# A fused recurrence and mixture-of-experts block on one core: decoder and output biases seeded by ScalarE, a router on differences of logits, experts in pairs, and a new order of stages

## The reference, cut to what matters

```python
xn = layernorm(x)
# s: the recurrence, one step per subsampled token
x_sub = rmsnorm(xn[:, ::2]) * g_norm
x_proj, gate = split(x_sub @ w_in.T + b_in)
h = tanh(h * A + x_proj[t][:, :, None] * Bm)        # h: (4, 512, 64), 2048 steps
y = h @ Cm.sum(0) + Dv * x_proj[t]
s = (y * silu(gate)) @ w_out.T + b_out
# g: the expert branch, on the same xn
cont = sigmoid(xn @ W_enc + b_enc) @ W_s2c + b_s2c  # 64 wide
top-2 of 8 experts by softmax(cont @ Wr + br), their weights renormalised
expert_out = sum_e gate_e * (relu(cont @ W1_e + b1_e) @ W2_e + b2_e)
g = silu(layernorm(sigmoid(expert_out @ W_c2s + b_c2s) @ W_dec + b_dec) * ln_g + ln_b)
out = x + s * g
```

## Time and profile before

| | us |
|---|---|
| median of 3 runs (6344.37 to 6348.86) | 6344.98 |
| the profiled execution | 6343.27 |
| its span, first to last instruction | 6341.6 |
| TensorE busy | 6147.9 (97%) |
| VectorE busy | 5732.7 (90%) |
| GpSimd busy | 5613.0 (89%) |
| ScalarE busy | 3988.1 (63%) |
| mean granted TensorE clock | 0.988 of full |

### The profile page before, as it was taken

One profiled execution on the slowest core, in us unless ns is written; L12 is line 12 of the kernel. 1 busy time (PEld: TensorE's weight loads), 2 busy tenths in 40 slices (PEclk: granted clock), 3 DMA queues, 4 the chain that ended last, 5 costly groups with the idle time before them and its releaser, 6 DMA issues.

```text
span 6341.6 us, 89178 instructions
## 1 busy us (share of the span) xinstructions
PE 6147.9 (97%) x29376; PEld 3202.8 (51%) x29376; DVE 5732.7 (90%) x10060; ACT 3988.1 (63%) x8390; POOL 5613.0 (89%) x3276
## 2 busy tenths in 40 slices
PE   5999999999999999999999999999999999999998
PEld 3555545555555455455554554555545545555554
DVE  4999999999999999999999999999999999999997
ACT  3666666666666666666666666666666666666665
POOL 4988989989889889899898898998988989989987
PEclk9999999999999999999999999999999999999999
DMA  5444444444434444444344444443444444444443
GB/s 144 104 110 99 110 105 104 110 102 107 110 99 110 105 103 110 102 107 112 97 110 106 103 113 102 105 113 95 109 108 102 114 101 106 112 96 110 109 102 80
DMA packets 157799, 672.95 MB, mean 106 GB/s; under 512 B 45589, under 2 KB 46613, under 8 KB 91799
## 3 DMA queue, kind: packets, MB, share of 16 engines
q1 hardware_dynamic: 157336, 667.24, 42.5%
HBM read 616.73 MB, written 50.33 MB: 105 GB/s over the span
## 4 chain that ended last, share of the span: by engine, by line
PE 91%; DVE 3%; POOL 3%; ACT 1%; issue 1%; SPq 1%; DMA 0%; POOLq 0%; DVEq 0%
PE bank L844 17%; PE bank L793 14%; PE ps_y L760 14%; PE ps_acc L856 9%; PE ps_acc L899 7%; PE bank L899 7%; PE bank L780 7%; PE bank L920 3%; PE bank L878 3%; PE bank L832 2%; POOL u L498 1%; PE bank L891 1%; PE ps_acc L891 1%; PE ps_acc L805 1%; PE ps_acc L878 1%
## 5 line engine op out<-in xcount | busy, mean ns | idle before, releaser
L498 POOL TENSOR_TENSOR u<-xb,bt 128x1024 f32<-128x1024 f32 x2048 | 4831.7, 2367 | 535.2 <-DVE ps_z L996 521.3
L600 ACT ACTIVATE h<-ps_z 128x512 f32<-128x512 f32 x4096 | 2377.1, 602 | 1280.0 <-DVE ps_z L996 1208.3
L990 DVE TENSOR_TENSOR ps_z<-h,ps_A 128x512 f32<-128x512 f32 x4096 | 2673.9, 691 | 416.0 <-ACT h L600 369.5
L996 DVE TENSOR_TENSOR ps_z<-ps_z,u 128x512 f32<-128x512 f32 x4096 | 2660.6, 691 | 8.7 <-POOL u L498 8.7
L844 PE MATMUL bank<-wide,w 65*128 65x256 f32 x4096 | 1138.8, 403 | 7.6
L760 PE MATMUL ps_y<-h,c_wide 128*32 128x512 f32 x8192 | 986.5, 599 | 0.0
L844 PEld LDWEIGHTS bank<-wide,w 65*128 65x128 f32 x4096 | 698.9, 189 | 454.6 <-issue 320.2
L793 PE MATMUL bank<-xnT,w_enc 128*128 128x256 f32 x4096 | 920.9, 383 | 6.5 <-ACT wide L623 6.5
L793 PEld LDWEIGHTS bank<-xnT,w_enc 128*128 128x128 f32 x4096 | 769.7, 190 | 213.0 <-issue 106.1
L681 ACT ACTIVATE hT<-bank 128x512 f32<-128x512 f32 x1024 | 604.1, 598 | 384.0 <-PE bank L844 366.6
L856 PE MATMUL ps_acc<-hT,w 128*64 128x256 f32 x4096 | 668.0, 404 | 6.7
(11 more groups left out here) (107 smaller groups left out, 4295.7 us busy)
## 6 DMA issues: line engine op xcount, KB each, us to landing
xb<-x_proj_scratch SPq DMA_DIRECT2D x2048, 256.0 KB, 4.5
xbuf<-in_L_attn_x SPq DMA_DIRECT2D x256, 128.0 KB
xres<-in_L_attn_x SPq DMA_DIRECT2D x512, 64.0 KB
out<-g SPq DMA_DIRECT2D x256, 128.0 KB
x_proj_scratch<-xp SPq DMA_DIRECT2D x256, 64.0 KB
w_in<-in_L_attn_w_in SPq DMA_DIRECT2D x1, 2048.0 KB
w_enc<-in_L_ffn_W_enc SPq DMA_DIRECT2D x1, 2048.0 KB
w_dec<-in_L_ffn_W_dec SPq DMA_DIRECT2D x1, 2048.0 KB
```

The costliest lines, as they stand in the source:

```text
L498: pool.tensor_tensor(u[:, tau % 2, :, :], xt, bt[:, :, :], ALU.mult).then_inc(u_ready, 1)
L600: act.activation(h[:, tau % RING, f, :], ps_z[:, f, :], ACT.Tanh).then_inc(h_ready, 1)
L990: dve.tensor_tensor(ps_z[:, f, :], h[:, (tau - 1) % RING, f, :], ps_A[:, f, :], ALU.mult).then_inc(m_done, 1)
L996: dve.tensor_tensor(ps_z[:, f, :], ps_z[:, f, :], u[:, tau % 2, f, :], ALU.add).then_inc(z_ready, 1)
```

## The change

Three pieces of work are done in another way, and most slots of the tables move.

1. `dec_seed` (ScalarE, slots 25 and 26) and `out_seed` (slot 37) copy the bias, now held on all 128 partitions, into the PSUM bank; the matmuls of `decode` and `fin_out` add to it, and their three bias matmuls are gone. TensorE waits for the seed.
2. `w_r` holds all 64 differences of the columns of `Wr` and the identity beside them. The router is one matmul of 128 columns per half of the tokens; its bias is one matmul of 256 columns over one row, issued in `controller` ahead of the sum. The copy of the logits is gone, and VectorE's routing has eight instructions instead of twelve, most of them of 64 columns.
3. `experts(p)` issues two ups, then the two downs of the pair before. The results of four `relu` are kept instead of two (the other two in the room of `conte`).
4. The tables: TensorE takes `gateT_transpose` ahead of the `conteT` ones, the others keep their order; VectorE, ScalarE, GpSimd and SyncE get other slots.

```diff
-SP_RESIDUAL = (36, 48)
+SP_RESIDUAL = (35, 47)
-POOL_GATE_MUL = -3
+POOL_GATE_MUL = -1
-POOL_FIN_SKIP = 31
-POOL_FIN_GATE = 36
-POOL_FIN_ADD = (53, 59)
+POOL_FIN_SKIP = 29
+POOL_FIN_GATE = 37
+POOL_FIN_ADD = (56, 62)
-ACT_LOGITS_COPY = 6.5
-ACT_ROUTE_SIG = 9.5
+ACT_ROUTE_SIG = 8.5
-ACT_DEC_SIG = (35.5, 39)
+ACT_DEC_SIG = (35.0, 38.5)
+ACT_OUT_SEED = 37
+ACT_DEC_SEED = (25, 26)
-PE_ROUTER = 8
-PE_CONTET = (17, 17, 18, 18)
-PE_GATET = 18
-PE_EXPERTS = (19, 19, 19, 19, 19, 19, 19, 19, 19, 19, 19, 20, 22, 22, 24, 28, 28)
-PE_TO_SPIKES = (31, 31, 31, 31)
+PE_ROUTER = 7
+PE_CONTET = (16, 17, 18, 18)
+PE_GATET = 15
+PE_EXPERTS = (19, 19, 19, 19, 19, 20, 22, 24, 28)
+PE_TO_SPIKES = (29, 29, 29, 29)
-DVE_PROJ_EVAC = (-21.25, -20.25)
-DVE_ROUTE = (7.25, 7.5, 7.75, 7.75, 8, 8.25, 9, 9.75)
-DVE_ROUTE_GATE = 10
-DVE_DEC_STATS = (28.75, 31.75)
-DVE_DEC_CENTRE = (30.75, 36.75)
+DVE_PROJ_EVAC = (-21.5, -20.5)
+DVE_ROUTE = (7.25, 7.5, 7.75, 8, 8, 8.25)
+DVE_ROUTE_GATE = 9.0
+DVE_DEC_STATS = (28.75, 31.0)
+DVE_DEC_CENTRE = (30.0, 36.75)
-DVE_FIN_Y = 34.75
-DVE_FIN_MUL = 40.5
+DVE_FIN_Y = 35.5
+DVE_FIN_MUL = 40.25
...
+            def dec_seed(blk, q):
+                if q == 0:
+                    wait_drained(act, (blk, C2S_FILL[1]))
+                else:
+                    act.wait_ge(acc_drained, 2 * blk + 1)
+                act.activation(dec_out[q][:, :], b_dec_all[:, :], ACT.Copy).then_inc(dec_seeded, 1)
+            def out_seed(blk):
+                wait_free(act, fin_fill(blk, FILL_FIN + 1))
+                act.activation(bank[1][:, :], b_out_all[:, :], ACT.Copy).then_inc(out_seeded, 1)
...
+                pe.matmul(ps_acc[:, T2:T2 + 2 * (E * E + M)], ones[96:97, :], br_row, start=True, stop=True)
...
                 for q in range(2):
                     tokens = contT[:, P * q:P * q + P]
-                    pe.matmul(logit_acc[:, q, :], ones[64:65, :], bias_rows[64:65, 0:E], start=True, stop=False)
-                    pe.matmul(logit_acc[:, q, :], tokens, w_r[:, :], start=False, stop=True)
-                    ins = pe.matmul(cont_acc[:, q, :], tokens, ident_2[:, :], start=True, stop=True)
+                    ins = pe.matmul(routed[:, q, :], tokens, w_r[:, :], start=False, stop=True,
+                                    skip_group_check=True)
...
-            def experts(blk, n):
-                if n < 16:
-                    expert_up(blk, n)
-                if n > 0:
-                    expert_down(blk, n - 1)
+            def experts(blk, p):
+                if p < 8:
+                    expert_up(blk, 2 * p)
+                    expert_up(blk, 2 * p + 1)
+                if p > 0:
+                    expert_down(blk, 2 * p - 2)
+                    expert_down(blk, 2 * p - 1)
...
             def decode(blk, q):
-                if q == 0:
-                    wait_free(pe, (blk, FILL_DEC))
-                else:
-                    pe.wait_ge(acc_drained, 2 * blk + 1)
+                pe.wait_ge(dec_seeded, 2 * blk + q + 1)
-                pe.matmul(dst[:, :], ones[0:1, :], bias_rows[0:1, :], start=True, stop=False)
...
             def fin_out(blk):
-                wait_free(pe, at)
-                pe.matmul(bank[1][:, :], ones[32:33, :], bias_rows[32:33, :], start=True, stop=False)
+                pe.wait_ge(out_seeded, blk + 1)
```

More of the change, by code:

```diff
@@ L154, in build @@
         ident = sb("ident", [P, P])
-        ident_2 = sb("ident_2", [P, M])
-        before = sb("before", [P, E, E])
+        least = sb("least", [P, E, E])
         c_wide = sb("c_wide", [P, F, 2 * SP - 4])
@@ L176, in build @@
         sg = sb("sg", [P, D])
-        logit = sb("logit", [P, 2, E])
         sel = sb("sel", [P, 2, E])
-        over = sb("over", [P, 2, E, E])
-        top_sum = sb("top_sum", [P, 2])
+        ahead = sb("ahead", [P, 2, E, E])
+        behind = sb("behind", [P, 2, E])
         gate = sb("gate", [P, 2, E])
@@ L207, in build @@
         gateT_acc = ps_acc[0:E, 0:T2]
[L208 to L216, removed]
+        routed = ps_acc[:, T2:T2 + 2 * (E * E + M)].rearrange("p (q n) -> p q n", q=2)
+        lead = [routed[:, q, 0:E * E].rearrange("p (e j) -> p e j", e=E) for q in range(2)]
+        cont_acc = routed[:, :, E * E:E * E + M]
+        rank = ps_acc[:, 0:16].rearrange("p (q e) -> p q e", q=2)
+        weight = ps_acc[:, 16:32].rearrange("p (q e) -> p q e", q=2)
         weights_loaded = sem("weights_loaded")
@@ L742, in between @@
                 for q in range(2):
+                    if slot == ACT_DEC_SEED[q]:
+                        dec_seed(blk, q)
+                for q in range(2):
                     if slot == ACT_DEC_SIG[q]:
                         dec_sig(blk, q)
+                if slot == ACT_OUT_SEED:
+                    out_seed(blk)
                 if slot == ACT_FIN_EVAC:
@@ L793, in encode @@
                         ins = pe.matmul(bank[n % 2][:, T2 * half:T2 * half + T2], w_enc[:, k, P * m:P * m + P],
-                                        xnT[:, par, k, :, :], start=(k == 0), stop=(k == KD - 1))
+                                        xnT[:, par, k, :, :], start=(k == 0 and half == 0), stop=(k == KD - 1),
+                                        skip_group_check=True)
                 filled(ins, at)
@@ L878, in to_spikes @@
                     ins = pe.matmul(dst[:, T2 * half:T2 * half + T2], w_c2s[:, P * m:P * m + P],
-                                    eoT, start=True, stop=True)
+                                    eoT, start=(half == 0), stop=True, skip_group_check=True)
                 if at:
@@ L961, in between @@
                     gateT_transpose(blk)
-                for n in range(17):
+                for n in range(9):
                     if slot == PE_EXPERTS[n]:
@@ L1018, in proj_evac @@
                                                  op0=ALU.mult, op1=ALU.add), at)
-            others = logit_acc.unsqueeze(2).to_broadcast([P, 2, E, E])
-            own = logit[:, :, :].unsqueeze(3).to_broadcast([P, 2, E, E])
-            earlier = before[:, :, :].unsqueeze(1).to_broadcast([P, 2, E, E])
             def route(blk, n):
                 if n == 0:
-                    dve.wait_ge(logits_copied, blk + 1)
+                    dve.wait_ge(logits_ready, blk + 1)
                     for q in range(2):
-                        dve.tensor_tensor(atleast[:, q], others[:, q], own[:, q], ALU.is_ge)
-                        ins = dve.tensor_tensor(over[:, q], others[:, q], own[:, q], ALU.is_gt)
+                        ins = dve.tensor_tensor(ahead[:, q], lead[q], least[:, :, :], ALU.is_ge)
@@ L1047, in route @@
-                if n == 7:
-                    ins = dve.scalar_tensor_tensor(out=margin, in0=logit_acc, scalar=2.0,
-                                                   in1=top_sum[:, :].unsqueeze(2).to_broadcast([P, 2, E]),
-                                                   op0=ALU.mult, op1=ALU.subtract)
+                    ins = dve.tensor_reduce(behind[:, :, :], ahead[:, :, :, :], AX.X, ALU.add)
                 ins.then_inc(route_steps, 1)
@@ L1129, in between @@
                         proj_evac(blk, par, half)
-                for n in range(8):
+                for n in range(6):
                     if slot == DVE_ROUTE[n]:
```

86 lines of the change are left out of this document (49 added, 37 removed).

## The result

The changed kernel takes **6539.67 us** (median of 4 runs, 6526.6 to 6556.09), the kernel before 6346.64 (4 runs, 6344.37 to 6348.86). The ratio is 1.0305, with a 95% interval of 1.028 to 1.0331. It is slower, where 6125 and a chance of 0.94 for faster had been forecast. The profiled execution took 6526.6 us.

A forecast was written before the change was run, and what follows sets the result against it. TensorE's matmuls were taken to set the pace, VectorE's recurrence close behind. Legs of 24.6, 20.6 and 48.7 us gave 93.9 per block against 97.35: 221 us saved over 64 blocks, 2 lost at the start, so 6125 us, range 5990 to 6225.

The forecast's parts named there:

- the one in the rivals: Clock rival, chance 0.04: TensorE's idle places bring 1.2 GHz stretches, 1.0 us each; six per block give 6508 us.
- leg A: Block part from the end of `dec_norm(1)` to the first `expert_up`: 26.0 us was to become 24.6.
- leg B: Block part from the first `expert_up` to `relu` 12: 22.5 us was to become 20.6.
- `fin_mul` now waits for VectorE's own order instead: In leg A, TensorE finishes `fin_out` about 2 us earlier and VectorE's routing, about 0.8 us shorter, sets `fin_mul`.
- `fin_mul` is one quarter slot earlier, which costs nothing: In leg A, moving VectorE's `fin_mul` a quarter slot ahead was counted as 0 us.
- Leg C: Block part from `relu` 12 to the next end of `dec_norm(1)`, paced by the recurrence: 48.8 us was to become 48.7.
- The wait at slot 28.75: In Leg C, VectorE's 0.41 us wait for the decoder's output was to go.
- two gaps stand behind the seeds: In Leg C, each decoder seed between two tanh was to delay its step by 0.4 us, 0.8 in all.
- GpSimd's side instructions: `fin_skip`, `fin_add` and `gate_mul`, moved to slots 29 to 31 ahead of the next block's u: 0.2 us lost.
- The 2 us for loading the bias rows: At the kernel's start, two bias rows become 128 rows, 0.5 MB more to load: 2 us estimated.
- The likeliest case: Chance 0.69: the recurrence takes over in Leg C and partly leg A; 92.4 to 94.9 us per block, 6030 to 6190.
- TensorE's own saving: TensorE's work falls by 6.3 us per block of 97.35, from bias matmuls, router and paired experts; 403 us if nothing else bound.

The follow-up runs named there:

- experiment 1: The changed kernel with the expert pairing alone undone, experts one by one again: 6443.96 us, 1.0158 of the kernel before.
- 4: The kernel before with the experts two by two alone, with four relu buffers: 6481.2 us, ratio 1.021.
- 3: The changed kernel with the ups over all 128 rows instead of 65, expert 0's result being another one: 6280.01 us, 0.9899 of the kernel before.
- 5: The kernel before with the experts two by two and the ups over all 128 rows, added rows zero: 6204.16 us, ratio 0.9779.
- 2: The changed kernel with two unread 128-row matmuls, one ahead of each of the first two pairs of ups: 6278.24 us, 0.9897 of the kernel before.
- 6: The kernel before with only the three bias matmuls replaced by ScalarE's seeds: 6366.59 us, ratio 1.0035.
- 7: The kernel before with only the router on differences of logits, the bias matmuls of decode and fin_out staying: 6387.82 us, ratio 1.0069.
- 8: The changed kernel with two unread 128-row matmuls ahead of the experts and GpSimd's second dec_silu ahead of u of step 8: 6168.27 us, 0.9725 of the kernel before.
- Experiment 9: The kernel of 8 with the three seeds moved behind the second tanh (slots 24.5, 26.5, 37.5): 6129.18 us, 0.966 of the kernel before.
- the three last runs: GpSimd's second dec_silu moved ahead of u of step 8 in the kernel of 6, the kernel before and the kernel of 5: 6512.48, 6444.09 and 6325.41 us.

## Why the prediction was wrong
**The step that failed first** is the one in the rivals: "A stretch at 1.2 GHz cost 1.0 us in the earlier trace rows", "so from four such stretches per block on it decides". The mechanism was named, its price was that of a stretch of 3.4 us in leg A, and its cause was looked for in idle places of TensorE. The prediction's count of such stretches was not what happened either: a short block of the changed kernel has one. The stretch that decided is one of 30.7 us. It costs 14.5 us in leg B (35.1 against 20.6), with the 6.8-us stretch that mostly goes ahead of it 16.8 in one block of three or four, 283 us over the kernel. It lies where TensorE has no idle time. Its conditions are the pairing (experiments 1 and 4) together with the 65 rows of the ups (3 and 5), and two matmuls over 128 rows at the head of the stage prevent it (2). The price of a 3.4-us stretch depends on its place: 1.0 us over `fin_out`, 1.7 over the input projection (6 and 7), nothing over the controller of the changed kernel. With GpSimd's wait gone (8) it costs 0.7 there too (leg A 25.47 against 24.76). Without the pairs, and so without the long stretch, the change is still slower than the kernel before (6444 us, experiment 1): the steps under leg A failed by themselves. The forecast of 6508 in this rival is near the measured time by luck: it stands for six short stretches per block, and TensorE's idle places were not the condition.

**Leg A: 24.6 forecast, 26.18 measured.** The step was "`fin_mul` now waits for VectorE's own order instead". It waits for GpSimd's, up to 1.66 us. The prediction read one block of before, one with a stretch at 1.2 GHz, in which TensorE was last by 1.1 us; in the 28 without one GpSimd's `dec_silu` was, so that TensorE's two microseconds could give 1.1 in half of the blocks and nothing in the others. Experiment 8, with GpSimd's order mended, gives 24.76. A second step failed beside it: "`fin_mul` is one quarter slot earlier, which costs nothing". It puts both sums of step 8 behind the wait for GpSimd, where one had stood ahead. In blocks without a stretch `fin_mul` starts 10.5 us after `dec_norm(1)` before, 10.4 in the changed kernel, but the last sum of step 8 ends at 12.43 and 13.05. With the seeds or the router alone, where `fin_mul` keeps slot 40.5, it ends at 12.38 and 12.41, and leg A is 25.50 and 25.53 against 26.18. So the quarter slot cost about 0.6 us per block; no run moves it back by itself. The terms beside it were near: the seed of 256 columns takes 0.60 us to the next group (3024.38 to 3024.98; forecast 0.57), and the seed ahead of the controller's sum starts within 0.2 us of the end of `dec_norm(1)`.

**Leg B: 20.6 forecast, 20.63 measured** where the clock is up. 0.3 us per pair was forecast, 0.31 measured (4).

**Leg C: 48.7 forecast, 48.83 measured.** The wait at slot 28.75 is gone; two gaps stand behind the seeds, 0.31 us each where 0.4 was forecast; `dec_norm(0)` does not wait for the stores. Experiment 9 shows what the seeds' places cost altogether, 0.7 us. Not every term is confirmed by the agreement: without the pairs the leg is 49.24 (1), with the seeds alone 48.67 (6), with the pairs alone 48.24 (4), so the pairs gave 0.4 to 0.6 here where 0.2 was counted, and other parts of the change took as much back; which, no run shows. The forecast also took 0.2 us for GpSimd's side instructions and left it out of its sum, which would be 48.9.

**Two smaller terms.** The 2 us for loading the bias rows had no row behind it; the blocks start 2.45 us later. The likeliest case's lower gain was not the sum of its legs' bounds: 1.0 and 1.4 less 0.8 is 1.6 us, 95.75 per block and not 94.9.

**TensorE's own saving**, 6.3 us per block forecast: 94.91 busy in the undisturbed block before, 88.77 after, 6.1 less. It is real and almost none of it is on the path: it becomes TensorE's idle time (6.9 us per block, 2.0 before), because the recurrence in C and GpSimd in A pace the block.

**What stays open.** Why one block in three or four falls into the long stretch, while the instructions and nearly the gaps in the expert stage are the same. In the changed kernel 15 of the 17 have a stretch of 6.8 us over the transposes ahead of it, but in the fourth experiment 8 of 17 have none. In both kernels all 17 begin in the second pair of ups or in the matmuls directly behind it, and all end while `y` runs or at its end. Also whether it is the two pairs of ups in a row at the stage's head that bring the clock down and the mixture of 65 and 128 rows that holds it, or one of them for both: no run separates the fall from the staying. Further, what the new tables cost leg C, and the cost of GpSimd's order in the kernels with the seeds or the router alone.

## What to carry to other kernels
Before taking switches or full-size matmuls out of a stage of TensorE whose other matmuls use part of the rows, price the whole stage at 1.2 GHz, not one short stretch, and try a version with the rows filled by zeros: here they cost nothing and were worth 277 us with the pairs. Where an instruction waits for the bounding engine, count over all blocks who released it: here another engine was last in half of them, and then that engine's order has to move with the change. An instruction that waits should stand behind all work that does not need what it waits for; a quarter slot cost 0.6 us. A stage can be moved ahead on one engine only if what it reads is moved ahead too, as the traces of the three last runs show.

## What the runs showed of the hardware
TensorE can stay at 1.2 GHz while the profile shows it busy without a gap: 30.70 us of 30.70, granted clock 0.50. The Trainium skill, "TensorE: Matmul & The Clock Gate", Part 1, says that the throttled state is the default and that activity of the array releases it. If activity is read as the busy time of the profile, this trace does not agree. With ups over 128 rows in place of 65, in the same number and with the same columns, no such stretch appears over the experts (6204 against 6481 us in the kernel before, 6280 against 6540 in the changed one). In all 34 long stretches of the blocks compared (17 in each of two kernels) the clock came back while `y` ran or at its end; `y` is 16 records over 128 rows and 512 columns.

A 512-column ScalarE instruction put between two tanh cost the recurrence 0.31 us, half of its own 0.60.
